# Two kinds of maximum over partitions, the order of VectorE's work, and the first transfers, in a fused session-conditioned layer with an fp8-quantized linear layer

## The reference, cut to what matters

```python
# part one, per item b: T = 2048 columns, 128 channels, HID = 256
cmask = arange(128) < _lenS[b]
h   = gelu(W_sess[id[b]].T @ (x[b] * cmask) + b_sess[id[b]])      # exact gelu, [256, T]
o   = (W2.T @ h + b2) * (arange(T) < seq_len[b])                  # [128, T]
# part two, on all items together
w_scale = 448 / max|weight|;   w_q = fp8e4m3(weight * w_scale)    # weight [2048, 2048]
o_scale = 57344 / max|o|;      o_q = fp8e5m2(o * o_scale)
out = x + (o_q @ w_q.T) / o_scale / w_scale + bias
```

## Time and profile before

| what | us |
|---|---|
| median of 3 runs | 886.58 |
| profiled execution | 885.46 |
| its span | 883.70 |
| PE busy | 842.7 |
| POOL busy | 444.6 |
| DVE busy | 479.9 |
| ACT busy | 380.0 |

### The profile page before, as it was taken

How to read it: one execution, slowest core, us unless ns; L and a number is a source line. 1 busy time by engine, 2 the same in 40 slices (tenths; PEclk the granted TensorE clock), 3 DMA queues, 4 the chain that set the end, 5 groups by cost and what they waited for, 6 DMA issues and landing times.

```text
span 883.7 us, 10121 instructions
## 1 busy us (share of the span) xinstructions
PE 842.7 (95%) x3508; PEld 473.6 (54%) x3508; DVE 479.9 (54%) x499; ACT 380.0 (43%) x369; POOL 444.6 (50%) x199
## 2 busy tenths in 40 slices
PE   7699996999999999999499999999999999999998
PEld 4466664677667766775244444444444444444443
DVE  4899994788888888888223223233232333323332
ACT  4467774888888888885101011010110101111010
POOL 3443442899999999997252423324233242332421
PEclk9899997999999999999699999999999999999999
DMA  7899983766666777656657887878878778787883
GB/s 249 301 373 352 356 336 140 271 257 252 252 252 258 275 280 274 256 203 234 205 176 261 238 289 248 286 245 261 288 247 290 243 261 287 247 291 243 261 272 109
DMA packets 104892, 230.20 MB, mean 261 GB/s; under 512 B 69272, under 2 KB 71200, under 8 KB 82464
## 3 DMA queue, kind: packets, MB, share of 16 engines
q1 hardware_dynamic: 104864, 229.85, 74.8%
HBM read 144.37 MB, written 69.21 MB: 242 GB/s over the span
## 4 chain that ended last, share of the span: by engine, by line
PE 86%; DVE 7%; issue 4%; DMA 2%; POOL 1%; ACT 1%; SPq 0%; DVEq 0%; ACTq 0%; POOLq 0%
PE ps_h L742 49%; PE ps_h L685 17%; PE ps_o L701 10%; PE ps_o L696 9%; DVE w_max L577 2%; DVE o_sb L546 1%; DVE hl L536 1%; DMA steps<-x_sb 1%; DVE o_max L549 1%; PE ps_h L719 1%; POOL xl L370 1%; DMA lens_i<-in_itok_B 0%; DVE whl L512 0%; DVE whl L515 0%; DVE xl L526 0%
## 5 line engine op out<-in xcount | busy, mean ns | idle before, releaser
L742 PE MATMUL ps_h<-wqT,steps 128*128 128x512 bf16 x1024 | 225.5, 381 | 1.0 <-DVE o_sb L638 0.8
L742 PE MATMUL ps_h<-wqT,x_sb 128*128 128x512 bf16 x1024 | 223.6, 379 | 0.0
L484 ACT ACTIVATE x_sb<-x_sb 128x2048 bf16<-128x2048 fp8e5 x31 | 59.2, 1910 | 361.6 <-DVE x_sb L615 361.6
L370 POOL TENSOR_TENSOR xl<-x_sb,xh 128x1024 fp32r<-128x1024 f32 x62 | 149.7, 2415 | 89.9 <-ACT xh L415 82.5
L685 PE MATMUL ps_h<-xh,whl 128*128 128x512 f32 x512 | 161.0, 436 | 16.7 <-DVE hl L536 16.3
L742 PEld LDWEIGHTS ps_h<-wqT,steps 128*128 128x128 bf16 x1024 | 100.3, 98 | 123.7 <-issue 3.8
L742 PEld LDWEIGHTS ps_h<-wqT,x_sb 128*128 128x128 bf16 x1024 | 100.2, 98 | 120.8 <-issue 1.0
L405 POOL TENSOR_TENSOR wt<-wt,bias_sb 128x2048 f32<-128x2048 f32 x16 | 72.2, 4515 | 143.3 <-DMA wt<-in_x 143.3
L405 POOL TENSOR_TENSOR h<-h,bias_sb 128x2048 f32<-128x2048 f32 x16 | 72.2, 4516 | 137.9 <-DMA h<-in_x 137.9
L685 PEld LDWEIGHTS ps_h<-xh,whl 128*128 128x128 f32 x512 | 96.7, 191 | 68.7 <-issue 47.6
L638 DVE SCALAR_TENSOR_TENSOR o_sb<-ps_h,scales,wt 128x512 f32<-128x512 f32 x64 | 47.9, 750 | 157.0 <-PE ps_h L742 148.7
(11 more groups left out here) (64 smaller groups left out, 617.0 us busy)
## 6 DMA issues: line engine op xcount, KB each, us to landing
masked_out<-o_sb SPq DMA_DIRECT2D x32, 1024.0 KB, 4.7
o_in<-masked_out SPq DMA_DIRECT2D x32, 1024.0 KB, 9.2
x_sb<-in_x SPq DMA_DIRECT2D x31, 1024.0 KB, 4.8
out<-o_sb SPq DMA_DIRECT2D x31, 1024.0 KB, 5.2
wqT<-in_L_ffn_weight SPq DMA_DIRECT2D x16, 1024.0 KB, 8.1
wt<-in_x SPq DMA_DIRECT2D x16, 1024.0 KB, 7.3
h<-in_x SPq DMA_DIRECT2D x16, 1024.0 KB, 7.3
wt<-in_L_ffn_weight SPq DMA_DIRECT2D x46, 352.0 KB, 4.9
```

What stands on the lines that cost most here:

```text
L370: pool.tensor_tensor(xl[:, u % 2, :], x_cols(u), xh[:, u % 2, :].bitcast(fp32), ALU.subtract)\
L742: mm = nc.tensor.matmul(ps_y[n], qT[r][:, k, :], wq[:, n, k, :], start=(k == 0), stop=(k == KT - 1))
```

## The change

It has these parts. The names are those of the code.

- **Maxima.** Both `partition_all_reduce` go. In their place PE multiplies the column of 128 row maxima (as the stationary operand) by a 128 x 128 identity, which lays it out as one row of 128 in PSUM; DVE reduces that row to one number; PE multiplies a row of 128 ones by it, which gives the number to all 128 partitions in PSUM. The four small steps of the weight scale (clip, reciprocal, product, reciprocal; L588 to L594) are now `weight_scale()`, at the head of turn 18. Waits for these stand in PE's list in slots 17 and 18.
- **VectorE's order.** In a turn the scan comes after `hl` instead of before it. The masked session weights of items 2 and 3 move to turns 0 and 1, after `hl`, that of item 1 behind `hl(0)`. `raw_sb` (4 buffers in `o_in`) and `whl` (4 buffers instead of 2) free these from waiting. The rounding of the last chunks moves behind the quantizing of item 0; no `round_at` stands in turn 63 or ahead of the last masks.
- **Chunks.** 736 columns instead of 704, so 45 chunks instead of 47; the exponent tile has 23 rows of 32 columns (with 2 spare) instead of 11 rows of 64.
- **First transfers.** The session numbers come by a transfer of their own (1 x 32, no broadcast), first of all; each other vector has a semaphore of its own, and the broadcast `ids` and `b_sess`, `lens` and `b2` come later. `hidden_bias` moves behind `hidden(0, 0)`.
- **Units 0 and 1.** `hidden(1, 0)` writes `ps_o[:, 1]` and stands ahead of slot 0. `hidden` takes the high half of the weight first.
- **PE's tail.** 24 matmuls without a use become 8, 2 and 4, around the two products of the `o` maximum.

```diff
-    CHUNK, CROWS = 704, 11
+    CHUNK, CROWS = 736, 23
-    WARM_START, WARM_MIDDLE = 2, 24
+    WARM_START = 2
+    WARM_SCALE, WARM_STEP, WARM_QUANT = 8, 2, 4
-        whl = sb("whl", [P, 2, 2 * HID], fp32r)
+        whl = sb("whl", [P, DIRECT, 2 * HID], fp32r)
+        raw_sb = [o_in[:, 0, b * HID:(b + 1) * HID] for b in range(DIRECT)]
...
+        def h0_of(u):
+            return ps_o[:, 1, :] if u == 1 else ps_h[:, 0, :]
+        w_row, w_all = ps_o[0:1, SCANS % 2, 0:P], ps_o[:, SCANS % 2, P:P + 1]
+        o_row, o_all = ps_h[0:1, 1, 0:P], ps_h[:, 1, P:P + 1]
...
-            for dst, src in ((ids_i, ids), (counts_i, counts), (lens_i, lens)):
-                sp.dma_start(dst[:, :], src.partition_broadcast(P)).then_inc(ids_loaded, 16)
-            sp.dma_start(bs_sb[:, :], b_sess).then_inc(bs_loaded, 16)
+            sp.dma_start(sid_i[:, :], ids.rearrange("(a b) -> a b", a=1)).then_inc(sid_loaded, 16)
+            sp.dma_start(counts_i[:, :], counts.partition_broadcast(P)).then_inc(counts_loaded, 16)
             load_x_part(0)
-            sp.wait_ge(ids_loaded, 48)
+            sp.wait_ge(sid_loaded, 16)
             load_session_weight(0)
+            sp.dma_start(ids_i[:, :], ids.partition_broadcast(P)).then_inc(ids_loaded, 16)
+            sp.dma_start(bs_sb[:, :], b_sess).then_inc(bs_loaded, 16)
             load_x_part(1)
             sp.dma_start(w2_sb[:, :, :], w2.rearrange("(j p) s -> p j s", p=P)).then_inc(params_loaded, 16)
             load_session_weight(1)
             load_x(1)
+            sp.dma_start(lens_i[:, :], lens.partition_broadcast(P)).then_inc(lens_loaded, 16)
+            sp.dma_start(b2_sb[:, :], b2.rearrange("(p a) -> p a", a=1)).then_inc(params_loaded, 16)
+            for b in range(2, DIRECT):
+                load_session_weight(b)
             sp.dma_start(sess_raw, w_sess.rearrange("s p k -> p s k")).then_inc(sess_loaded, 16)
...
+            pool.memset(ones[:, :], 1.0).then_inc(steps_ready, 1)
-                if u == SCANS + 1:
-                    pool.wait_ge(w_pmax_ready, 1)
-                    pool.partition_all_reduce(w_amax, w_pmax, P, bass.bass_isa.ReduceOp.max)
-            pool.wait_ge(o_pmax_ready, 1)
-            pool.partition_all_reduce(o_amax, o_pmax, P, bass.bass_isa.ReduceOp.max).then_inc(o_amax_ready, 1)
...
...
+            def split_session_weight(b):
+                dve.wait_ge(raw_loaded[b], 16)
+                mask = cmask[:, b:b + 1]
+                dve.tensor_scalar(whl[:, b, 0:HID], raw_sb[b], mask, None, ALU.mult).then_inc(wh_direct, 1)
+                dve.wait_ge(wh_direct, b + 1)
+                dve.scalar_tensor_tensor(whl[:, b, HID:2 * HID], raw_sb[b], mask,
+                                         whl[:, b, 0:HID].bitcast(fp32), ALU.mult, ALU.subtract).then_inc(wl_direct, 1)
...
+            dve.tensor_copy(xh[:, 0, :], x_cols(0)).then_inc(xh_ready, 1)
+            split_session_weight(0)
...
             split_h_rest(0)
+            split_session_weight(1)
+            dve.wait_ge(lens_loaded, 16)
...
             for u in range(UNITS):
+                if u == SCANS + 2:
+                    weight_scale()
                 if u >= 1:
...
                     mask_o(u - 1, start, 0, slice(0, UNIT))
-                if u == 1 or u == 3:
-                    mask_session_weight((u + 3) // 2)
-                if 1 <= u <= SCANS:
...
+                if 0 <= u - QUANT - 1 < CHUNKS and u + 1 < UNITS:
+                    round_at(u - QUANT - 1)
                 if u == SCANS + 1:
                     dve.wait_ge(w_scanned, SCANS)
                     dve.tensor_reduce(w_pmax, w_max[:, :], AX.X, ALU.max).then_inc(w_pmax_ready, 1)
-                if 0 <= u - QUANT - 1 < CHUNKS:
-                    round_at(u - QUANT - 1)
                 if u + 1 < UNITS:
                     split_h_rest(u + 1)
+                if u < DIRECT - 2:
+                    split_session_weight(u + 2)
+                if 1 <= u <= SCANS:
+                    scan(u - 1)
                 if u == SCANS + 1:
+                    dve.wait_ge(w_row_psum, 1)
+                    dve.tensor_reduce(w_one[:, :], w_row, AX.X, ALU.max).then_inc(w_one_ready, 1)
-                    dve.wait_ge(w_amax_ready, 1)
...
-            if UNITS - QUANT - 1 < EARLY:
-                round_at(UNITS - QUANT - 1)
             for k, cols in enumerate(HALVES):
                 mask_o(UNITS - 1, start, k, cols)
...
             hidden(0, 0)
+            hidden_bias()
             hidden(0, 1)
+            hidden(1, 0)
             for u in range(UNITS - 1):
-                hidden(u + 1, 0)
+                if u > 0:
+                    hidden(u + 1, 0)
+                if u == SCANS + 2:
+                    pe.wait_ge(scale_step, 1)
                 project0(u, HALVES)
+                if u == SCANS + 1:
+                    pe.wait_ge(w_pmax_ready, 1)
+                    nc.tensor.matmul(w_row, w_pmax, ident_f[:, :], start=True, stop=True).then_inc(w_row_psum, 1)
                 hidden(u + 1, 1)
                 project1(u, HALVES)
+                if u == SCANS + 1:
+                    pe.wait_ge(w_one_ready, 1)
+                    nc.tensor.matmul(w_all, ones[:, :], w_one[:, :], start=True, stop=True).then_inc(w_amax_psum, 1)
...
-            for k in range(WARM_MIDDLE):
-                nc.tensor.matmul(ps_y[0], wq[:, 0, 0, 0:P], wq[:, 0, 0, :], start=True, stop=True)
+            pe.wait_ge(w_rounded, 1)
+            stay_warm(WARM_SCALE)
+            pe.wait_ge(o_pmax_ready, 1)
+            nc.tensor.matmul(o_row, o_pmax, ident_f[:, :], start=True, stop=True).then_inc(o_row_psum, 1)
+            stay_warm(WARM_STEP)
+            pe.wait_ge(o_one_ready, 1)
+            nc.tensor.matmul(o_all, ones[:, :], o_one[:, :], start=True, stop=True).then_inc(o_amax_psum, 1)
+            stay_warm(WARM_QUANT)
             pe.wait_ge(o_masked, UNITS + 1)
```

More of the change, by code:

```diff
@@ L84, in adaln_ffn @@
         ident = sb("ident", [P, P], fp8)
+        ident_f = sb("ident_f", [P, P], fp32)
+        ones = sb("ones", [1, P], fp32)
+        w_one = sb("w_one", [1, 1], fp32)
+        o_one = sb("o_one", [1, 1], fp32)
         w_max = sb("w_max", [P, SCANS], fp32)
         o_max = sb("o_max", [P, UNITS + 1], fp32)
[L87 to L89 removed]
+        scales = sb("scales", [P, 11], fp32)
+        w_pmax, w_clip, w_rec, w_scale, w_inv = (scales[:, k:k + 1] for k in range(5))
+        o_pmax, o_clip, o_rec, o_scale, o_inv, y_scale = (scales[:, k:k + 1] for k in range(5, 11))
         wqT = sb("wqT", [P, WCOLS], bf16)
@@ L147, in adaln_ffn @@
         onehot_ready = sem("onehot_ready")
+        ident_ready = sem("ident_ready")
         hbias_psum = sem("hbias_psum")
@@ L151, in adaln_ffn @@
         x_first = [sem(f"x_first{p}") for p in range(UPB)]
+        raw_loaded = [sem(f"raw_loaded{b}") for b in range(DIRECT)]
         wraw_loaded = [sem(f"wraw_loaded{r}") for r in range(2)]
@@ L276, in _ @@
                 b = u // UPB
-                if u == 0:
-                    for n in range(2, DIRECT):
-                        sp.wait_ge(wl_direct, n - 1)
-                        load_session_weight(n)
                 if u % UPB == 0 and b + 2 < B:
@@ L619, in _ @@
                 quantize(0, 1, k == 0, CUT[k])
-            for i in range(UNITS - QUANT, CHUNKS):
+            for i in range(UNITS - 2 - QUANT, CHUNKS):
                 round_at(i)
@@ L679, in hidden @@
                     pe.wait_ge(h1_gelu, u)
-                for k, (part, xs) in enumerate(((1, xh), (0, xh), (0, xl))):
+                for k, (part, xs) in enumerate(((0, xh), (1, xh), (0, xl))):
                     rows = slice(part * HID + t * P, part * HID + (t + 1) * P)
+                    if k == 1 and t == 0 and b < DIRECT and u % UPB == 0:
+                        pe.wait_ge(wl_direct, b + 1)
                     if k == 2 and t == 0:
@@ L716, in _, with stay_warm @@
                 project1(UNITS - 1, [cols])
-            for k in range(WARM_MIDDLE):
-                nc.tensor.matmul(ps_y[0], wq[:, 0, 0, 0:P], wq[:, 0, 0, :], start=True, stop=True)
+            def stay_warm(count):
+                for k in range(count):
+                    nc.tensor.matmul(ps_y[0], wq[:, 0, 0, 0:P], wq[:, 0, 0, :], start=True, stop=True)
+            pe.wait_ge(w_rounded, 1)
[6 more added lines that the diff above has]
+            stay_warm(WARM_QUANT)
             pe.wait_ge(o_masked, UNITS + 1)
```

154 lines of the change are left out of this document (74 added, 80 removed).

## The result

| | before | after |
|---|---|---|
| median, us | 886.69 (885.62 to 888.06) | 854.58 (854.46 to 856.10) |
| profiled execution | 885.46 | 854.56 |
| its span | 883.70 | 852.80 |

The ratio is 0.9644 (95%: 0.9632 to 0.9657). The forecast was 857 with a range of 848 to 866. Between the two profiled executions 30.9 us went. I read after in the order in which before was read.

What follows compares the result with a forecast made beforehand. PE's own work bounds most of the kernel; waits can be won. 7.7 (stages A to C) + 8.0 (Stage D) + 12.9 (Stage F) + 0.9 (clock) = 29.5 us off 885.46 gives 856.0, median 857, range 848 to 866.

Steps and rivals of the forecast that it cites:

- Stage B: Slots 2 and 3: VectorE's masked session weight waits for GpSimd; the stall moves to slot 3, 6.3 us instead of 7.6.
- Stage C: Scans, slots 4 to 17: with `hl` ahead of the scan each slot takes 5.89 us, 0.2 us less.
- Stage D: Weight maximum, slots 18 and 19: without `partition_all_reduce` 8.0 us gained, bounds 6.5 to 8.8; PE loses 2.0 to 2.3.
- Stage F: Maximum of `o`, after PE's last projection: 12.9 us gained, from 2.90 of roundings moved and 11.37 shrinking to 1.3.
- stages A to C: From the start to slot 18, which begins at 128.0 instead of 135.63: 7.7 us gained together.
- Stage A: Start: 1.9 us gained at slot 1, 0.9 by an earlier first gelu, 1.0 by `hidden(1, 0)` ahead of slot 0.
- Rival 1: Slots 2 and 3: VectorE is not blocked by GpSimd, slot 3 follows at once; 7.7 us more, 849; 10%.
- Rival 2: Scans: transfers bind, slots stay at 6.10 us, 2.9 us lost and a late x, 860 to 861; 13%.
- Stage E: Rounding, with 45 chunks of 736 columns for 47 of 704: nothing gained, idle time hides the longer steps.
- Rival 4: Rounding's second step comes to need GpSimd's port, its tile having another shape; 49 us slower, 906; 4%.
- The clock: Item 0 of part two, behind the `o` maximum: shorter PE idleness raises the granted clock from 0.50, 0.9 us gained.
- Rival 3: Around `o`: the last item's store or x load replaces the wait, half of Stage F stays, 864; 7%.

Runs made afterwards that it cites:

- e7: The kernel before with the chunk part alone: 736 columns, 45 chunks, the last rounded behind item 0's quantizing, both maxima still on GpSimd: 871.65 us.
- e9: The changed kernel with the gelu table loaded ahead of ACT's wait for the hidden bias, and w2's split no longer waiting for `b2`: 853.29 us.
- e4: The changed kernel with item 3's session weight split in turn 0, right behind item 2's, instead of in turn 1: 850.27 us.
- e5: e4 plus scans 2 and 3 issued ahead of SP's wait for the split session weights, scan 4 ahead of its wait for their store: 848.07 us.
- e3: The changed kernel with the scan back ahead of `hl` in VectorE's turn, nothing else: 857.44 us.
- e1: The changed kernel with the weight maximum alone back on GpSimd (`partition_all_reduce`, no products): 863.63 us.
- e6: The changed kernel with `hidden` taking the low half of the session weight first, as before: 855.38 us.
- e8: The changed kernel with chunks of 704 columns again (47 chunks), the last three behind the quantizing: 867.78 us.
- e10: The changed kernel with 16 rows instead of 23 in the exponent tile, same 736 columns: 879.61 us.
- e2: The changed kernel with the maximum of `o` alone back on GpSimd, without its two products, chunk work and 14 unused matmuls kept: 856.97 us.
- e11: The changed kernel without the 14 unused matmuls around the products of the `o` maximum: 856.96 us.

## Why the prediction was right, and where it wasn't

**The whole.** 857 against 854.58 is right, by the mechanism forecast in stages B, C and D. Stage F has the right size for partly the wrong reason. It came out right because the change holds both parts, which is luck as far as the mechanism goes: for the chunk part alone the same sum gives 883.4, and 871.65 was measured (e7). (By the prediction's own numbers stages A to C are 135.63 - 128.0 = 7.6, not 7.7; nothing hangs on it.)

**Stage A** is mis-sized: 1.3 us at slot 1 (21.84 to 20.55), 1.9 forecast. The term that failed is the first gelu: 12.77 to 12.56, 0.2 us, where 0.9 was forecast (11.9). The product for the hidden bias starts at 9.82 (9.5 forecast) and takes 1.06 us for the 0.60 I used; the copy and the table load behind it are as I put them. The other term, 1.0 us for `hidden(1, 0)` ahead of slot 0, came (1.29 - 0.21 = 1.1). Windows of after:

```profile
9.90:16.00 6.10, 6.10 (x16) 4.64 (x16) 3.31 (x6) 5.06 (x7) 0.00 (x0) 0.50 0.91 311
16.00:18.00 2.00, 2.00 (x10) 1.62 (x10) 1.93 (x4) 2.00 (x3) 1.31 (x1) 1.00 1.08 416
```

From 9.9 to 16 us PE runs at the lower clock (0.50, the 1.2 GHz level), after it had been idle from 5.24 to 7.21. e9 shows 1.2 us more to be had at slot 1 once the table load and the wait for `b2` are off the path. What fixes the first pace isn't settled: the four records of `hidden(0, 1)` take 2.08 us in e9 as well, where the granted clock reads 1.00.

**Stage B** is right step by step: slot 2 at 26.36 (26.1 forecast), `hl` of slot 3 ready at 38.45 (38.2), slot 3 at 38.60 (38.3). That the blocked pair makes the stall was argued in the prediction; e4 shows it by moving the pair alone. Slot 3 then took 7.67, not 7.20: after PE's wait the granted clock was 0.50 to 41 us and 0.62 to 44, and in the slot behind the old stall 0.50 and 0.90. Rival 1 (849) needed the pair to miss GpSimd's split, which it did not; e4 and e5 are what it would have looked like.
The Trainium skill ("SBUF — State Buffer", section "Who interferes with whom") says that the second comer is blocked for the whole instruction. Trace and e4 agree: 4.04 us for 0.34.

**Stage C** is right (e3: 6.18 us a slot with the old order, 5.87 with the new). Rival 2 is refuted: with the transfers at 97% and 383 GB/s PE has no gap, so the 94% of the earlier trace rows was no limit.
The Trainium skill's figure ("SBUF — State Buffer", "Summary: rules for kernel authors") of about 358 GB/s is exceeded by the 383 measured over 76 us; the measurement decides.

**Stage D** is right in size and mechanism (8.2 for 8.0; e1 gives back 9.0, 8.3 expected). PE loses 2.0 us in slots 17 and 18 together (136.36 - 122.62 - 2 x 5.87; 2.0 to 2.3 forecast).

**Stage E.** Nothing was forecast, 0.9 us came. e6 excludes the order of halves. The chunks are excluded too: from slot 20 to PE's last projection before with the new chunks (e7) takes 256.88 us, after with the old ones (e8) 256.02. I have no run that shows the cause, it stays open. Rival 4 was rightly given little for this kernel: L572 takes 536 ns in the median and 539 at most with 736 columns, against 520 and 521 with 704, so it never waits. e10 shows that its premise about parity of rows was the right thing to ask.

**Stage F** is where a step failed, though the sum held: "11.37 us become two products (0.3 each), a reduce and the steps between engines". The steps after the row maximum do take 1.3 us as put there. But the 11.37 us were not the price of the reduction. With GpSimd free, the reduction costs 2.1 us more than the products (e2: 0.4 of wait, 1.7 of slower matmuls), and the chunk work alone wins 14.0 (e7). The prediction gave that move 2.90 us, by VectorE's row. VectorE did win that (row maximum 5.69 us after PE's last projection before, 2.80 after), but I didn't look at GpSimd's rows: its last rounding ended at 421.94, 1.7 us behind the row maximum, and only then did the gap of 9.25 us begin. The two parts are two cures for one wait. What the products alone would win, with the rounding left in place, was not run; by the rows of before my estimate is up to 11.37 - 1.3 = 10.1 us. With the move made they are worth 2.1 in e2; and e7, whose 24 fillers keep item 0 at 13.97 us, stands only 6.23 - 5.42 = 0.8 us behind after in this stretch. The clock is mis-sized, 2.0 us for 0.9: the granted clock is 1.00 from PE's last projection on (0.50 in the earlier trace rows), which e11 shows to be the fillers' doing.

**Rival 3** is refuted: neither store nor `x` load stands behind PE's 5.42 us. In e8, where the last store is issued 10 us later, VectorE does wait for it and 5.77 us reach PE: the rival named a wait that exists, but it does not bind in after.
